# Second layer of a four-layer attention program: its weights split in twelve parts, eight of them during its first round, and two loads issued during the first layer

## The chip, the cores and the metric

The program runs on one core of a Trainium2 chip. The metric is device time in microseconds: the median over repeated executions of the whole program. TensorE is written PE, VectorE DVE, ScalarE ACT, GpSimd POOL and SyncE SP, as the profile does. All loads of this kernel are issued from SP's queue.

## What is computed

Four attention layers follow one another on `x` of shape 16 x 128 x 256, with a context of the same shape. The change is at the start of the second layer (and in what the first layer loads). Cut from the reference, the second layer is:

```python
# z: x after layer one; u: the context; both 16 x 128 x 256, split in two column halves s:e of 128
h = einsum('od,bdl->bol', Wqkv_i, z[:, :, s:e]) + einsum('od,bdl->bol', Winj_i, u[:, :, s:e])
q, k, v = split(concatenate(chunks, axis=2), 3, axis=1)      # 16 heads of 64
score = einsum('bndi,bndj->bnij', q + r_w_bias, k) * SCALE
prob = softmax(score)
attn_vec = einsum('bnij,bndj->bndi', prob, v)
x = einsum('od,bdl->bol', Wo, attn_vec) + bo + z
x = (x - mean(x)) * rsqrt(var(x) + eps)                      # over the 128 channels
```

`Wqkv_i` and `Winj_i` (i = 0, 1) are four matrices of 3072 x 128, 1.5 MB each.

## The kernel before, in words

`program` runs three blocks one after the other, with a barrier between them: `layer0` (layer one), `layer1` (layer two) and `layers23`.

**Layer one** (`layer0`) is a software pipeline over eight pairs of batches. At its start SP issues, in this order (L379 to L390): the first pair's `x_in`, `cols`, `wqkv`, `rows` (broadcast to 128 partitions), `self_mul`, `cT`, `cross_mul`, the other weights, and then three of the four big matrices of layer two: `wz0_raw`, `wz1_raw`, `wi0_raw`. After these it issues `x_in` of pair 1 (`next_x`, L365 to L368), as soon as POOL has made `x_ao` of pair 0 (L436). On DVE the statistics of `x_in` (L824) stand in a fixed order among the score operations (L901, L906); the normalisation `ln` (L837), the copies `vm` (L852) and the transposes of `ln` on PE (L509) come after them.

**Layer two** (`layer1`) works in rounds of two batches, eight rounds, each with sixteen steps (eight pairs of heads times two batches). PE multiplies in a two-term form: every operand of a projection is a rounded high part (suffix `h`, type fp32r, made by ACT) and the remainder (suffix `l`, input minus high part, made by DVE). So before the first projection the weights have to be split: `parts` (L1102) lists eight pieces, the first halves (1536 columns) of the four matrices and then their second halves. ACT rounds them in that order (L1414), DVE subtracts in the same order (L1550), and after the fourth piece both do the same for the context tile `ub` (L1384, L1467). The remainder is written over the raw weight's place (`wz0_raw` and `wzl0` are the same memory).

The fourth matrix, `wi1_raw`, and the first `ub` are loaded by SP at the start of the second layer (L1177 to L1180). Of PE:

```python
for name in AHEAD:          # "q0", "k0", "v0b0"
    pe.wait_ge(lo_made, len(parts) // 2 if name in ("q0", "k0") else len(parts))
    project(0, name)
rounds(pe, body, tail)
```

`project` (L1217) is 12 matmuls for each name: two column halves, times `z` and `u`, times three products of high and remainder parts. The results go to two PSUM banks in turn (`work`, class `Banks`), so `v0b0` waits until DVE has read `q0` out of its bank (`rest_work`, L1454), and the first `scores` (L1235) wait for `k0` (L1458).

A step `t` of a round, in each engine's own order, is written out in the four `body` functions:

- PE (L1309): `scores(t)`, `times_v(t-2)`, `turn(t-1)`, every other step `times_wo`, then the projections listed in `FILLS[t]` (L1112) for later heads.
- ACT (L1389): two exponentials of step t (L1352), `copy_turned(t-1)` (L1361), `round_heads(t-2)` (L1367), the high parts of the projections (L1372, L1375).
- DVE (L1506): `maxima` of both heads (L1427), `copy_turned(t-1)` (L1438), `inverse_sums` (L1433), `rest_heads(t-2)` (L1443), the remainders of the projections (L1454, L1458) or the copy of `v` (L1449).
- POOL (L1199): `norm(t, 0)` and `norm(t, 1)`, which multiply the probabilities by the inverse sums (L1192). PE's `turn(t)` in step t+1 (L1258) waits for them.

The first round has its own unrolled code (`body(0, first=True, ...)`). Before it POOL makes the remainder of `wo` (L1210).

## Time and profile before

| | us |
|---|---|
| median of 3 runs | 1376.34 (1374.86 to 1376.57) |
| the profiled execution's own time | 1375.4 |
| its span, first to last instruction | 1373.7 |
| PE busy | 1246.0 (91%) |
| DVE / ACT / POOL busy | 942.0 / 837.2 / 497.7 |
| last PE instruction of layer one ends | 495.5 |
| first PE instruction of layer two | 506.77 |
| first scores of layer two | 516.42 |

Times inside the trace are microseconds from the start of the span. A row of the timeline has the start, the duration, the engine, the line of the kernel, the operation, what it writes and reads, how many instructions are merged in it, and in brackets how long the engine had been idle and who ended the wait. Back-to-back instructions of one engine overlap a little, so n of them take less than n times the duration of one.

### The profile page before, as it was taken

What the parts mean: (1) busy time and instruction counts of PE and PEld (TensorE: products, weight loads), DVE (VectorE), ACT (ScalarE), POOL (GpSimd) and SP (SyncE); (2) the same over time, 40 slices, a digit from 0 to 9 for tenths busy, and PEclk for the clock granted to TensorE, in tenths of its full rate; (3) what the DMA queues carried; (4) which work ended last, traced back from release to release, by engine and by line L of the source; (5) the groups of instructions that cost most, each with busy time, mean ns of one, the idle gap of its engine ahead of it and who ended that gap; (6) DMA issues with size and microseconds to landing.
All of it is one profiled execution on the core that took longest, in us unless ns stands there. A gap on an engine that the chain in (4) does not pass through costs nothing. (4 is left out here: it accounts for less than half of the span.)

```text
span 1373.7 us, 31155 instructions
## 1 busy us (share of the span) xinstructions
PE 1246.0 (91%) x10866; PEld 1011.5 (74%) x10866; DVE 942.0 (69%) x1843; ACT 837.2 (61%) x2494; POOL 497.7 (36%) x490
## 2 busy tenths in 40 slices
PE   3788999898998749999999999999999999995997
PEld 2667777787787648888888888888888888882554
DVE  2777978879787566666666766666666666662554
ACT  2688877887886545555555555555655556552453
POOL 2455555445544103333333333333333333342000
PEclk9899999999999979999999999999999999997999
DMA  8000000000000020000000000000000000000100
GB/s 312 9 14 20 10 21 8 11 11 16 5 13 1 1 77 1 2 9 1 2 9 0 8 0 0 9 0 0 8 0 9 0 0 1 1 1 26 46 31 31
DMA packets 18547, 24.96 MB, mean 18 GB/s; under 512 B 1360, under 2 KB 16912, under 8 KB 18064
## 3 DMA queue, kind: packets, MB, share of 16 engines
q1 hardware_dynamic: 18448, 23.77, 5.1%
q8 instruction: 46, 0.75, 0.2%
q14 instruction: 53, 0.43, 0.1%
HBM read 21.67 MB, written 2.10 MB: 17 GB/s over the span
## 5 line engine op out<-in xcount | busy, mean ns | idle before, releaser
L1192 POOL TENSOR_TENSOR prob<-prob,l_z_inv 128x512 f32<-128x512 f32 x256 | 261.0, 1040 | 457.1 <-DVE l_z_inv L1433 457.1
L1352 ACT ACTIVATE prob<-psum,l_neg_max 128x256 f32<-128x256 f32 x512 | 235.6, 473 | 245.9 <-DVE l_neg_max L1427 231.9
L741 ACT ACTIVATE ring_e<-ring_e,neg_max 128x128 f32<-128x128 f32 x512 | 164.7, 410 | 15.1 <-DVE neg_max L906 15.0
L1427 DVE TENSOR_REDUCE l_neg_max<-psum 128x2 f32<-128x512 f32 x256 | 164.0, 682 | 10.6 <-PE psum L1246 10.6
L1258 PEld LDWEIGHTS psum<-ident,prob 128*128 128x128 f32 x1024 | 109.8, 141 | 49.0 <-issue 45.4
L1274 PE MATMUL psum<-pT,vs 128*64 128x256 f32 x1024 | 138.8, 391 | 6.7 <-DVE aTl L1443 6.5
L1258 PE MATMUL psum<-ident,prob 128*128 128x128 f32 x1024 | 140.0, 280 | 0.0
L1438 DVE COPY pT<-psum 128x512 f32<-128x512 f32 x128 | 88.2, 689 | 51.1 <-PE psum L1258 51.0
L448 POOL TENSOR_TENSOR ring_e<-ring_e,cross_add 128x512 f32<-128x512 f32 x64 | 83.2, 1308 | 95.2 <-DVE ring_e L901 95.2
L448 POOL TENSOR_TENSOR ring_e<-ring_e,self_add 128x512 f32<-128x512 f32 x64 | 85.4, 1348 | 81.5 <-DVE ring_e L901 80.8
L1443 DVE TENSOR_TENSOR aTl<-psum,aTh 128x256 fp32r<-128x256 f32 x128 | 54.4, 425 | 73.9 <-ACT aTh L1367 73.9
L749 ACT COPY ring_t<-psum 128x512 f32<-128x512 f32 x128 | 75.1, 587 | 48.0 <-PE psum L592 47.3
L1352 ACT ACTIVATION_READ_ACCUMULATOR prob<-psum,l_neg_max 128x1 f32 x512 | 104.0, 203 | 0.0
L1274 PEld LDWEIGHTS psum<-pT,vs 128*64 128x64 f32 x1024 | 63.2, 136 | 42.9 <-issue 5.9
L592 PE MATMUL psum<-ident,ring_e 128*128 128x128 f32 x512 | 83.8, 289 | 8.8 <-ACT ring_t L749 8.8
L1246 PE MATMUL psum<-kh,qh 64*128 64x256 f32 x512 | 85.8, 332 | 4.1 <-ACT prob L1352 4.1
L906 DVE TENSOR_REDUCE neg_max<-ring_e 128x4 f32<-128x512 f32 x128 | 84.7, 666 | 2.0 <-POOL ring_e L448 2.0
L1228 PE MATMUL psum<-zuh,wzh 128*128 128x256 f32 x256 | 74.4, 291 | 11.3 <-DVE zul L1469 11.3
L592 PEld LDWEIGHTS psum<-ident,ring_e 128*128 128x128 f32 x512 | 63.6, 148 | 24.8 <-issue 10.3
L912 DVE RECIPROCAL z_inv<-psum 128x256 f32<-128x256 f32 x32 | 56.1, 1753 | 33.7 <-PE psum L619 33.5
L1361 ACT COPY pT<-psum 128x512 f32<-128x512 f32 x128 | 76.4, 597 | 2.3 <-PE psum L1258 2.3
L1228 PE MATMUL psum<-zuh,wih 128*128 128x256 f32 x256 | 72.8, 284 | 0.0
(197 smaller groups left out, 3226.9 us busy)
## 6 DMA issues: line engine op xcount, KB each, us to landing
wz_raw<-wz_in SPq DMA_DIRECT2D x2, 1536.0 KB, 14.4
x_in<-x SPq DMA_DIRECT2D x8, 256.0 KB, 2.8
cT<-ctxT SPq DMA_DIRECT2D x8, 256.0 KB, 2.9
w<-w_in SPq DMA_DIRECT2D x2, 1024.0 KB, 11.6
l_ub<-ctx_in SPq DMA_DIRECT2D x8, 256.0 KB, 2.7
cg<-ctx_in SPq DMA_DIRECT2D x4, 512.0 KB, 3.7
out<-fin SPq DMA_DIRECT2D x4, 512.0 KB, 2.8
wi_raw<-wi_in SPq DMA_DIRECT2D x1, 1536.0 KB, 17.2
```

The costliest lines, as they stand in the source:

```text
L448: pool.tensor_tensor(e, e, add, ALU.add).then_inc(scores_add.sem, 1)
L592: last = nc.tensor.transpose(turn_bank[:, h * P:(h + 1) * P], ring_e[:, n % RE, h * P:(h + 1) * P], ident[:, :])
L741: last = nc.scalar.activation(e, e, ACT.Exp, bias=neg_max[:, n % RE, h:h + 1])
L906: nc.vector.tensor_reduce(neg_max[:, n % RE, :], ring_e[:, n % RE, :].rearrange("p (h k) -> p h k", h=QUAD), AX.X, ALU.max, negate=True).t ...
L1192: pool.tensor_tensor(e, e, z_inv[:, t % RE, h, :].unsqueeze(2).broadcast_to([P, 2, D]), ALU.mult)\
L1228: last = mm(o, w[wp][c][:, at:at + P], zu[xp][:, s, c, :, :].rearrange("p b l -> p (b l)"), **flags)
L1246: last = mm(score_bank[h][:, qt * D:(qt + 1) * D], q[qp][rows, pair % 2, qt, b, :], k[kp][rows, pair % 2, :, b, :], start=(qp, kp) == (0, ...
L1258: last = nc.tensor.transpose(turn_bank[h][:, kt * D + qt * P:kt * D + (qt + 1) * P], prob[:, t % RE, h, qt * D + kt * P:qt * D + (kt + 1) ...
L1274: last = mm(pv_bank[h * HD1:(h + 1) * HD1, :], vs[:, pair // 2 % 2, b, kt, at:at + HD1], pT[:, h, kt * D:(kt + 1) * D], start=kt == 0, sto ...
L1352: last = nc.scalar.activation(prob[:, t % RE, h, qt * D:(qt + 1) * D], score_bank[h][:, qt * D:(qt + 1) * D], ACT.Exp, bias=neg_max[:, t % ...
L1427: nc.vector.tensor_reduce(neg_max[:, t % RE, h, :], score_bank[h].rearrange("p (t c) -> p t c", t=2), AX.X, ALU.max, negate=True).then_inc ...
L1438: nc.vector.tensor_copy(pT[:, 1, :], turn_bank[1]).then_inc(copied[1].sem, 1)
```

## The change

1. **Loads.** The fourth big matrix (`wi1_raw`, 1.5 MB) joins the other three at the start of layer one, ahead of `x_in` of pair 1. The first `ub` is loaded at the end of SP's list in layer one. To make room, `rows` loses its last 256 columns (its load goes from 1536 to 1280 columns in each of 128 partitions). SP issues neither in layer two any more.
2. **Splitting by parts.** The weights are split in 12 parts of 256 columns of each of the four matrices (`PARTS`): `qk` parts hold the `q` and `k` columns of one pair of heads, `v` parts the columns of four heads. Four parts (`AT_ONCE`) are made before the first round, the other eight in its steps: ACT rounds part t+4 at the end of step t (t = 0 to 7), POOL subtracts its two `wi` pieces after the norms of step t, DVE subtracts its two `wz` pieces in step t+1, between the maxima and `copy_turned`.
3. **Who subtracts.** The remainders of the two `wi` matrices move from DVE to POOL. The two counters are `z_lo_made` and `i_lo_made`.
4. **Who waits.** In the first round every `project` waits for both counters to reach its own part (`rounded`).

```diff
-            for w, src, c in ((wz0_raw, "wz_in", 0), (wz1_raw, "wz_in", 1), (wi0_raw, "wi_in", 0)):
+            for w, src, c in ((wz0_raw, "wz_in", 0), (wz1_raw, "wz_in", 1), (wi0_raw, "wi_in", 0),
+                              (wi1_raw, "wi_in", 1)):
                 sp.dma_start(w[:, :], v[src][c * P:(c + 1) * P, :]).then_inc(l1_weights_in, 16)
...
-            sp.dma_start(rows[:, :], v["rows_in"].partition_broadcast(P)).then_inc(w_rows, 16)
+            sp.dma_start(rows[:, :], v["rows_in"][0:ROWS["bvpg"]].partition_broadcast(P)).then_inc(w_rows, 16)
...
             sp.wait_ge(w_mask, 16)
-            sp.wait_ge(l1_weights_in, 48)
+            sp.dma_start(v["ub"][:, :, :], v["ctx_in"].rearrange("b p d -> p b d")[:, 0:2, :])\
+                .then_inc(v["first_u_in"], 16)
+            sp.wait_ge(l1_weights_in, 64)
+            sp.wait_ge(v["first_u_in"], 16)
...
+        PARTS = ["qk0", "v0", "qk1", "qk2", "v1", "qk3", "qk4", "v2", "qk5", "qk6", "v3", "qk7"]
+        AT_ONCE = 4
+        tensors = ((wz[0][0], wz[1][0], wz0_raw), (wz[0][1], wz[1][1], wz1_raw),
+                   (wi[0][0], wi[1][0], wi0_raw), (wi[0][1], wi[1][1], wi1_raw))
...
-            load_u(0)
-            for h in range(2):
-                sp.dma_start(wi1_raw[:, h * HALF:(h + 1) * HALF],
-                             v["wi_in"][P:2 * P, h * HALF:(h + 1) * HALF]).then_inc(wi_in, 16)
-                sp.wait_ge(wi_in, 16 * (h + 1))
...
+            def rest_part(n):
+                for m, (hi, lo, raw) in enumerate(tensors[2:4]):
+                    pool.wait_ge(hi_made, len(tensors) * n + m + 3)
+                    pool.tensor_tensor(part(lo, n), part(raw, n), part(hi, n).bitcast(F32), ALU.subtract)\
+                        .then_inc(i_lo_made, 1)
...
                     for h in range(2):
                         norm(i, t, h)
+                    if first and t < len(PARTS) - AT_ONCE:
+                        rest_part(t + AT_ONCE)
...
+                if isinstance(i, int) and i == 0:
+                    pe.wait_ge(z_lo_made, rounded(name))
+                    pe.wait_ge(i_lo_made, rounded(name))
...
+            def round_part(n):
+                for hi, lo, raw in tensors:
+                    nc.scalar.copy(part(hi, n), part(raw, n)).then_inc(hi_made, 1)
...
+                    if first and t + AT_ONCE < len(PARTS):
+                        round_part(t + AT_ONCE)
...
                     maxima(i, t, 1)
+                    if first and 0 < t <= len(PARTS) - AT_ONCE:
+                        rest_part(t - 1 + AT_ONCE)
                     if t >= L_T or not first:
                         copy_turned(i, t - L_T)
...
             rest_z(0)
-            for n, (hi, lo, raw) in enumerate(parts):
-                dve.wait_ge(hi_made, n + 1)
-                nc.vector.tensor_tensor(lo, raw, hi.bitcast(F32), ALU.subtract).then_inc(lo_made, 1)
-                if n == 3:
-                    rest_u(0)
+            rest_part(0)
+            rest_u(0)
+            for n in range(1, AT_ONCE):
+                rest_part(n)
```

**How the instructions move on ACT.** The start of layer two, from the rounding of `z` to the first projection read out (`qh`); `wzh`, `wih` are the high parts, `wz_raw`, `wi_raw`, `wil_raw` the weights as loaded. Before:

```order
L1381 CAST zuh<-xs 128x512
L1414 CAST wzh<-wz_raw 128x1536 [waits l1_weights_in]
L1414 CAST wzh<-wz_raw 128x1536
L1414 CAST wih<-wi_raw 128x1536
L1414 CAST wih<-wil_raw 128x1536 [waits l1_wi_in]
L1386 CAST zuh<-l_ub 128x512 [waits l1_u_in]
L1414 CAST wzh<-wz_raw 128x1536 x2
L1372 ACTIVATE qh<-psum,cols 128x512 [waits l1_work_bank0_full]
```

Now:

```order
L1410 CAST zuh<-xs 128x512
L1423 CAST wzh<-wz_raw 128x2x128 x2
L1423 CAST wih<-wi_raw 128x2x128 x2
L1418 CAST zuh<-l_ub 128x512 [waits first_u_in]
L1423 CAST wzh<-wz_raw 128x256 x2
L1423 CAST wih<-wi_raw 128x256 x2
L1401 ACTIVATE qh<-psum,cols 128x512 [waits l1_work_bank0_full]
```

Four casts of 256 columns stand ahead of the rounding of `ub` where four of 1536 did, the wait for `l1_wi_in` is gone, and 16 casts of 256 columns stand ahead of `qh` in all.

**On POOL**, from the barrier into layer two to the norms of the first steps. Before:

```order
L1210 TENSOR_TENSOR wol<-wol_raw,woh 128x1024 [waits wo_hi_made]
L1192 TENSOR_TENSOR prob<-prob,l_z_inv 128x512 [waits l1_z_inv_done] x18
L1197 TENSOR_TENSOR l_rstd<-l_var_eps,half_neg 128x4 [waits l1_work_bank1_read_out]
```

Now:

```order
L1219 TENSOR_TENSOR wil<-wi_raw,wih 128x2x128 [waits weights_hi_made] x2
L1219 TENSOR_TENSOR wil<-wi_raw,wih 128x256 [waits weights_hi_made] x2
L1219 TENSOR_TENSOR wil<-wi_raw,wih 128x2x128 [waits weights_hi_made] x4
L1237 TENSOR_TENSOR wol<-wol_raw,woh 128x1024 [waits wo_hi_made]
L1209 TENSOR_TENSOR prob<-prob,l_z_inv 128x512 [waits l1_z_inv_done] x2
L1219 TENSOR_TENSOR wil<-wi_raw,wih 128x256 [waits weights_hi_made] x2
L1209 TENSOR_TENSOR prob<-prob,l_z_inv 128x512 [waits l1_z_inv_done] x2
L1219 TENSOR_TENSOR wil<-wi_raw,wih 128x2x128 [waits weights_hi_made] x2
```

Eight subtractions stand ahead of the remainder of `wo`, and two after each pair of norms in steps 0 to 7.

**On DVE**, steps 1 and 2 of the first round (`l_neg_max` are the maxima, `pT` is `copy_turned`, `l_z_inv` the inverse sums). Before:

```order
L1427 TENSOR_REDUCE l_neg_max<-psum 128x2 [waits l1_scores_done] x2
L1438 COPY pT<-psum 128x512 [waits l1_pv_done,l1_turned]
L1433 RECIPROCAL l_z_inv<-l_z_sum 128x2 [waits l1_probs_done,l1_exp_done] x2
L1449 COPY vs<-psum 128x512 [waits l1_work_bank1_full]
L1454 SCALAR_TENSOR_TENSOR ql<-psum,cols,qh 128x512 [waits l1_work_hi]
```

Now:

```order
L1462 TENSOR_REDUCE l_neg_max<-psum 128x2 [waits l1_scores_done] x2
L1544 TENSOR_TENSOR wzl<-wz_raw,wzh 128x256 [waits weights_hi_made] x2
L1473 COPY pT<-psum 128x512 [waits l1_pv_done,l1_turned]
L1468 RECIPROCAL l_z_inv<-l_z_sum 128x2 [waits l1_probs_done,l1_exp_done] x2
L1484 COPY vs<-psum 128x512 [waits l1_work_bank1_full]
L1489 SCALAR_TENSOR_TENSOR ql<-psum,cols,qh 128x512 [waits l1_work_hi]
```

Two subtractions stand between the maxima and the inverse sums, in each of steps 1 to 8.

## Rows read from the trace of the kernel before

**Rows 1.** Stretches: length, PE PEld DVE ACT POOL busy, granted clock, DMA share, GB/s.

```profile
496.00:507.00 11.00, 0.23 (x1) 0.26 (x2) 8.55 (x8) 8.98 (x8) 0.00 (x0) 0.57 0.50 167
516.40:606.00 89.60, 88.34 (x769) 74.50 (x768) 62.01 (x131) 52.45 (x175) 33.60 (x33) 0.99 0.01 4
```

**Rows 2.** Timeline of layer two's start, up to its second projection read out.

```profile
496.33 0.62 ACT L1381 CAST zuh<-xs 128x512 fp32r<-128x512 f32 x1 [10.48 <-PEq L150]
496.86 2.84 ACT L1414 CAST wzh<-wz_raw 128x1536 fp32r<-128x1536 f32 x2
496.98 0.69 DVE L1464 TENSOR_TENSOR zul<-xs,zuh 128x512 fp32r<-128x512 f32 x1 [0.96 <-ACT zuh L1381]
...
506.77 0.55 PE L1228 MATMUL psum<-zuh,wzh 128*128 128x256 f32 x1 [11.28 <-DVE zul L1469]
...
511.88 0.60 ACT L1375 ACTIVATE kh<-psum 128x512 fp32r<-128x512 f32 x1 [1.05 <-PE psum L1228]
```

**Rows 3.** The same timeline, the second wait and the first steps.

```profile
513.49 2.38 POOL L1210 TENSOR_TENSOR wol<-wol_raw,woh 128x1024 fp32r<-128x1024 f32 x1 [35.93 <-ACT woh L1420]
513.88 0.68 DVE L1458 SCALAR_TENSOR_TENSOR kl<-psum,kh 128x512 fp32r<-128x512 f32 x1
514.07 0.36 PE L1232 MATMUL psum<-wzh,zuh 128*128 128x256 f32 x1 [2.22 <-DVE wil L1550]
...
518.00 0.41 PE L1228 MATMUL psum<-zuh,wzh 128*128 128x256 f32 x1
```

**Rows 4.** Stretches as in rows 1, around the second wait.

```profile
511.00:512.00 1.00, 0.85 (x6) 0.64 (x5) 1.00 (x2) 0.12 (x1) 0.00 (x0) 0.88 0.10 33
515.00:516.00 1.00, 1.00 (x6) 1.00 (x6) 0.00 (x0) 0.00 (x0) 0.87 (x1) 0.50 0.00 0
```

**Rows 5.** Single casts and subtractions: duration min/median/max in ns.

```profile
L1550 DVE TENSOR_TENSOR wzl<-wz_raw,wzh x4: 1750/1751/1759, 498.4 to 508.2; 128x1536 fp32r<-128x1536 f32 x4
L436 POOL TENSOR_TENSOR x_ao<-x_in,rows x8: 1265/1273/1275, 30.2 to 364.6; 128x512 f32<-128x512 f32 x8
```

**Rows 6.** DVE beside POOL: durations of one line, and the timeline of round seven.

```profile
L1464 DVE TENSOR_TENSOR zul<-xs,zuh x8: 693/1392/1512, 497.0 to 1141.3; 128x512 fp32r<-128x512 f32 x8
...
1140.12 2.04 POOL L1192 TENSOR_TENSOR prob<-prob,l_z_inv 128x512 f32<-128x512 f32 x2 [3.47 <-DVE l_z_inv L1433]
1141.32 1.39 DVE L1464 TENSOR_TENSOR zul<-xs,zuh 128x512 fp32r<-128x512 f32 x1 [0.22 <-ACT zuh L1381]
```

**Rows 7.** Step 2 of the first round: ACT, POOL and PE's turn after it.

```profile
528.09 0.47 ACT L1352 ACTIVATE prob<-psum,l_neg_max 128x256 f32<-128x256 f32 x1 [1.42 <-DVE l_neg_max L1427]
529.77 2.04 POOL L1192 TENSOR_TENSOR prob<-prob,l_z_inv 128x512 f32<-128x512 f32 x2 [3.07 <-DVE l_z_inv L1433]
532.39 1.09 PE L1258 MATMUL psum<-ident,prob 128*128 128x128 f32 x8
```

**Rows 8.** Loads of the first 34 us: KB each, us from issue to landing.

```profile
wi_raw<-wi_in SPq DMA_DIRECT2D x1, 1536.0 KB, 17.2
self_mul<-smask SPq DMA_DIRECT2D x1, 64.0 KB, 7.2
...
x_in<-x SPq DMA_DIRECT2D x1, 256.0 KB, 3.1
```

**Rows 9.** The start of layer one: timeline, and the DMA rate of one stretch.

```profile
16.71 0.43 SPq L390 DMA_DIRECT2D wi_raw<-wi_in  x1
28.00:30.00 2.00, 0.00 (x0) 0.00 (x0) 1.75 (x4) 0.26 (x1) 2.00 (x2) 0.99 1.03 436
31.53 28.78 SPq L354 DMA_DIRECT2D x_in<-x  x2
35.13 0.74 DVE L824 BATCH_NORM_STATS2 stats<-x_in 128x6 f32<-128x256 f32 x2
40.58 0.76 DVE L852 TENSOR_TENSOR vm<-psum,rows 128x256 f32<-128x256 f32 x2 [0.41 <-PE psum L527]
41.49 0.63 PE L509 MATMUL psum<-ident,ln 128*128 128x128 f32 x4 [0.57 <-DVE vm L852]
```

More of the change, by code:

```diff
@@ L101, in program @@
         half_neg = sb("half_neg", [P, 4])
+        ub = sb("l1_ub", [P, 2, D])
+        first_u_in = ctx.enter_context(nc.semaphore("first_u_in"))
         raw_place = ExitStack()
-        wz0_raw, wz1_raw, wi0_raw = (raw_place.enter_context(nc.sbuf_tensor(n, [P, 3 * NQ], F32)) for n in (
-            "wz0_raw", "wz1_raw", "wi0_raw"))
+        wz0_raw, wz1_raw, wi0_raw, wi1_raw = (raw_place.enter_context(nc.sbuf_tensor(n, [P, 3 * NQ], F32)) for n in (
+            "wz0_raw", "wz1_raw", "wi0_raw", "wi1_raw"))
         l1_weights_in = ctx.enter_context(nc.semaphore("l1_weights_in"))
@@ L134, in layer0 @@
         "psum", "xs", "ident", "mean_w", "cols", "half_neg", "col"))
-    (l1_weights_in, wz0_raw, wz1_raw, wi0_raw) = (v[n] for n in ("l1_weights_in", "wz0_raw", "wz1_raw", "wi0_raw"))
+    (l1_weights_in, wz0_raw, wz1_raw, wi0_raw, wi1_raw) = (v[n] for n in (
+        "l1_weights_in", "wz0_raw", "wz1_raw", "wi0_raw", "wi1_raw"))
     NB = 2
@@ L162, in event @@
             return e
-        rows = sb("rows", [P, len(ROWS) * D])
+        rows = sb("rows", [P, ROWS["bvpg"]])
         wqkv = sb("wqkv", [P, 2, 3 * D])
@@ L1044, in layer1 @@
         "sb", "psum", "xs", "ident", "mean_w", "half_neg", "col"))
-    (l1_weights_in, wz0_raw, wz1_raw, wi0_raw, wzl0, wzl1, wil0) = (v[n] for n in (
-        "l1_weights_in", "wz0_raw", "wz1_raw", "wi0_raw", "wzl0", "wzl1", "wil0"))
+    (wz0_raw, wz1_raw, wi0_raw, wi1_raw, wzl0, wzl1, wil0, wil1) = (v[n] for n in (
+        "wz0_raw", "wz1_raw", "wi0_raw", "wi1_raw", "wzl0", "wzl1", "wil0", "wil1"))
     NB = 2
@@ L1073, in place @@
             return raw, sb(name, shape, F32R)
-        wi1_raw, wil1 = place("wil1", [P, 3 * NQ])
         wo_raw, wol = place("wol", [P, PAIRS, P])
@@ L1099, in layer1, with part, rounded @@
         wo_bank = psum[:, 7, :]
[L1101 to L1104 removed]
+        PARTS = ["qk0", "v0", "qk1", "qk2", "v1", "qk3", "qk4", "v2", "qk5", "qk6", "v3", "qk7"]
+        AT_ONCE = 4
+        tensors = ((wz[0][0], wz[1][0], wz0_raw), (wz[0][1], wz[1][1], wz1_raw),
+                   (wi[0][0], wi[1][0], wi0_raw), (wi[0][1], wi[1][1], wi1_raw))
+        def part(w, n):
+            if PARTS[n][0] == "v":
+                return w[:, 2 * NQ + int(PARTS[n][1]) * D:2 * NQ + (int(PARTS[n][1]) + 1) * D]
+            at = int(PARTS[n][2]) * P
+            return w[:, 0:2 * NQ].rearrange("p (t c) -> p t c", t=2)[:, :, at:at + P]
+        def rounded(name):
+            n = "v" + name[1] if name[0] == "v" else "qk" + name[1]
+            return 2 * (PARTS.index(n) + 1)
         wo_hi, wo_lo, wo_in_place = (w[:, :, :].rearrange("p h o -> p (h o)") for w in (*wo, wo_raw))
[L1106 to L1108 removed]
+        wo_in = sem("l1_wo_in")
+        hi_made, z_lo_made, i_lo_made, wo_hi_made, wo_lo_made = (sem(n) for n in (
+            "weights_hi_made", "z_weights_lo_made", "i_weights_lo_made", "wo_hi_made", "wo_lo_made"))
         FILLS = [("q1", "k1"), ("v0b1", "q2"), ("k2",), ("v1b0", "q3"), ("k3", "v1b1"), ("q4", "mean"), ("k4",),
@@ L1207, in tail @@
                 inverse_std(i, "k0")
+            for n in range(AT_ONCE):
+                rest_part(n)
             pool.wait_ge(wo_hi_made, 1)
@@ L1341, in _ @@
             for name in AHEAD:
-                pe.wait_ge(lo_made, len(parts) // 2 if name in ("q0", "k0") else len(parts))
                 project(0, name)
@@ L1384, in round_u @@
             def round_u(i):
-                act.wait_ge(*u_in.at(i))
+                if isinstance(i, int) and i == 0:
+                    act.wait_ge(first_u_in, 16)
+                else:
+                    act.wait_ge(*u_in.at(i - 1))
                 nc.scalar.copy(zu[0][:, 1, :, :, :], ub[:, :, :].rearrange("p b (c l) -> p c b l", c=2))\
                     .then_inc(zu_hi.sem, 1)
+            def round_part(n):
+                for hi, lo, raw in tensors:
+                    nc.scalar.copy(part(hi, n), part(raw, n)).then_inc(hi_made, 1)
             def body(i, first, last):
@@ L1504, in output, with rest_part @@
                 nc.vector.tensor_tensor(to, y[:, b, :], ps, ALU.mult).then_inc(work.reads(name), 1)
+            def rest_part(n):
+                for m, (hi, lo, raw) in enumerate(tensors[0:2]):
+                    dve.wait_ge(hi_made, len(tensors) * n + m + 1)
+                    nc.vector.tensor_tensor(part(lo, n), part(raw, n), part(hi, n).bitcast(F32), ALU.subtract)\
+                        .then_inc(z_lo_made, 1)
             def body(i, first, last):
@@ L1547, in _ @@
             rest_z(0)
-            for n, (hi, lo, raw) in enumerate(parts):
-                dve.wait_ge(hi_made, n + 1)
-                nc.vector.tensor_tensor(lo, raw, hi.bitcast(F32), ALU.subtract).then_inc(lo_made, 1)
-                if n == 3:
-                    rest_u(0)
+            rest_part(0)
+            rest_u(0)
+            for n in range(1, AT_ONCE):
+                rest_part(n)
             for name in AHEAD:
```

22 lines of the change are left out of this document (7 added, 15 removed).

## Prediction

> **What bounds the kernel now.** I read first the stretches, then the timeline of the hand-over from layer one to layer two, then the first round step by step, and last the start of layer one, because a load was moved there. In the stretch of the first round PE is busy 88.3 of 89.6 us, with DVE at 62.0, ACT at 52.5 and POOL at 33.6 [rows 1]. So layer two is bound by PE once it runs, and a round has spare time on the other three. Before it, from 496 to 507, PE is busy 0.23 of 11 us [rows 1]. The reader is to see two waits there: 11.28 us until 506.77, behind the first four pieces of weights, the wait for `wi1_raw` and the context's remainder, and 2.22 us until 514.07, behind the last four pieces on DVE [rows 2, 3]. Both waits are on the path, since PE has nothing else. The second has an after-effect: the granted clock is 0.88 in 511 to 512 and 0.50 again in 515 to 516 [rows 4], 1.2 instead of 2.4 GHz, after the idle stretch from 511.88.
>
> **Prices of the small pieces.** A cast takes 0.62 us for 512 columns (L1381) and two of 1536 take 2.84 [rows 2], so one is 1.47 and the next starts after 1.37. The straight line through both gives 0.41 us for 256 columns, one every 0.31. On DVE 512 columns take 0.69 [rows 2] and 1536 take 1.75 [rows 5], so 256 take 0.42, one every 0.35. On POOL 512 columns with two full inputs take 1.27 [rows 5] and 1024 take 2.38 [rows 3], so 256 take 0.71.
>
> **Term 1: when PE starts.** ACT ends the first cast at 496.95 as now, and its next four are done at 497.27, 497.58, 497.89 and 498.20, the context's at 498.7; no load is waited for. Without any hindrance DVE would end the context's remainder at 499.4 and POOL its second piece at 499.3, and PE would start at 499.5 instead of 506.77. But DVE and POOL now subtract side by side, both with two SBUF inputs. The trace shows what that does: L1464 takes 693 ns at the least and 1392 in the median; at 1141.32 it starts under POOL's pair of norms (1140.12 to 1142.16) and ends 0.55 after the pair does [rows 6]. DVE stood still meanwhile. I therefore put these instructions one behind the other: from 497.6, two pieces on DVE (0.8), the context (0.69), two on POOL (1.42), 2.9 us in all, so PE starts at 500.5, 6.3 us earlier.
>
> The Trainium skill states this as a rule ("SBUF — State Buffer", section "SBUF: two separate sides"): a DVE instruction with two SBUF inputs and a GpSimd instruction take the shared port pair as an exclusive lock, and the later one blocks until the other has ended. The trace agrees (1392 ns beside 693 ns). By it term 1 is 6.3; an even sharing of time would leave up to 7.3.
>
> **Term 2: when the rounds start.** The second half of the wait falls away altogether or nearly. `q0` and `k0` take 5.1 us on PE as now (506.77 to 511.88) [rows 2], so they end at 505.6. `v0b0` waits until DVE has read `q0`, and DVE has six more pieces to do first, which alternate with six of POOL's: 6 x (0.38 + 0.71) = 6.5 us, to 507.0, DVE's last at 506.3. `ql` (0.75) then frees the bank at 507.1, `kl` (0.68) [rows 3] ends at 507.7, `v0b0` runs from 507.1 to 508.6 (24 matmuls in 5.1 us, mostly at half clock, are 0.21 each; my estimate at full clock is 0.12, so 12 take 1.5), the scores take 0.9 to 1.0, and `q1` starts at 509.6, where it starts at 518.00 now [rows 3]: **8.4 us earlier**. The lower bound is half clock through `v0b0` and the scores, as now: the 3.9 us from 514.07 to 518.00 [rows 3] in place of 2.5 gives 7.0. The upper bound is no lock at all: start at 499.5, `k0` at 504.6, `v0b0` at once to 506.1, scores, `q1` at 507.1, 10.9 earlier. I take 8.4, which goes by the row nearest to the case (rows 6). POOL then has the remainder of `wo` (2.38) from 507.0 to 509.4 and its first norm at about 511.6, so that is hidden.
>
> **Term 3: the eight parts inside the first round.** ACT gets four casts (1.3 us) at the end of steps 0 to 7. Before the exponentials of step 2 it idles 1.42 us [rows 7], and in the same view the other seven steps have about as much or more: it fits, by about 0.1. DVE gets 0.8 us between maxima and inverse sums in steps 1 to 8, plus the wait for POOL's two pieces, which become ready only just before: about 0.5. So the norms of a step come some 1.1 us later. Those of step 2 end at 531.81, and `turn` begins at 532.39 and needs the second head half of its 1.09 later, at 532.9 [rows 7]: 1.1 us late against 1.1 us of slack. In the same view this is the tightest of the eight steps. POOL idles 3.07 before these norms [rows 7] and its two pieces need 1.4. Nothing else of PE hangs on it: the parts are made at least one step before their projection. I take +0.3 us, with 0 and 3 as bounds (0.3 to 0.4 lost in each of eight steps, if the slack is used up). The work is the same number of columns; only its cover, PE's 99% busy round, is new. If that cover went, it would cost 8 x 1.3 us on ACT.
>
> **Term 4: the moved loads.** Layer two's own issues go (what ACT waited for them lies inside term 1), and the first `ub` is loaded while SP has nothing to do: 0. But `wi1_raw` is now queued ahead of `x_in` of pair 1. The rows show that what is queued is served behind what was issued before: `self_mul`, 64 KB, lands 7.2 us after its issue behind `rows`, and `wi_raw`, issued at 16.71, after 17.2 us, at 33.9 [rows 8, 9]. `x_in` is issued at 31.53 and lands 3.1 later, at 34.6; DVE takes it at 35.13 with no wait [rows 8, 9]. Now 1.57 MB more and 0.13 MB less (`rows`) stand before it, 1.44 MB at 436 GB/s [rows 9]: 3.3 us. It lands at about 38.0 and DVE's statistics are 2.9 late. Behind them on DVE stand the scores' masks and maxima, `ln` and `vm`, all in order. `vm` has 0.41 us of slack (it waited for PE), and PE waits 0.57 for it before the transposes at 41.49 [rows 9]. So PE is 2.5 late from there, and this pipeline only starts up: I find nothing later that it could catch up on. **+2.5 us.** Bounds: 0, if PE's work in hand covers it, and 4, if PE's longer idleness costs clock as well. That `self_mul` comes 0.4 us earlier behind the shorter `rows` does not help, since the wait for `x_in` follows.
>
> **Sum.** -8.4 + 0.3 + 2.5 = -5.6 us, from the profiled execution's 1375.4 to 1369.8. The median of the runs is 0.9 above that execution, so the median to come is 1376.3 - 5.6 = 1370.7. About 0.2% (2.75 us) is what a measurement tells from no change.
>
> **Rivals.**
> - *DVE and POOL do not hinder each other.* Then term 2 is 10.9 and the sum -8.1: 1368.2. For it: in the first pieces DVE is done before POOL starts, and pieces of 256 columns are short. Against it: rows 6. Chance 0.13.
> - *The late `x_in` costs nothing* (served earlier than I think, or caught up). Then the sum is -8.1 as well, 1368.2, or 1366 with the rival above. For it: `x_in` landed after 3.1 us although `wi_raw` was still under way. Against it: every load of this queue lands in its turn. Chance 0.15.
> - *Half clock at both places*: term 2 is 7.0, term 4 is 4, sum -2.7: 1373.6. For it: rows 4 show it once after a gap of 2.2 us; mine are 1.5 and some 2. Chance 0.15.
> - *Slower: POOL is the new bound.* Mechanism: a POOL piece of 256 columns (half of them as 2 x 128) costs as much as one of 512, 1.27. Then four parts at the start take 8 x 0.56 = 4.5 us longer, and in each of eight steps the norms come 2.2 us late; against 1.1 us of slack in the tightest and more in the others I count 0.6 us of PE each, 5 in all. Sum: -8.4 + 4.5 + 5 + 2.5 = +3.6, 1379.9. It decides from about 0.4 us of additional cost in each piece on. Against it: POOL's 1.27 and 2.38 lie on a line that leaves 0.16 for zero columns. Chance 0.05.
> - *The change does not do what it says*, because the second wait merely moves to DVE's backlog; that is inside term 2 and has been priced there.
>
> **Chances and range.** My forecast has 0.52, the rivals 0.13, 0.15, 0.15 and 0.05. Faster by over 0.2% are the forecast, the first two rivals and nearly half of the third: 0.86. Within 0.2%: 0.10; slower: 0.04. The range is 1366.3 to 1374.0: down to both fast rivals together, up to the half clock at both places.
>
> **What would show it.** In the changed profile: PE's first projection at about 500.5 + 2.5 = 503 (if it is 502, the lock is not there); POOL's pieces near 0.7 us or stretched by DVE's; `q1` about 6 us before 518.00; DVE idle before the statistics near 35 until `x_in` lands near 38, and layer one's last matmul at 498 instead of 495.5; the first round still 99% PE busy and no new wait of PE on POOL's norms. I am wrong if layer one ends where it did (term 4), if the time from layer one's end to `q1` shrinks by other than 8.4 (term 2), or if the first round takes over 1 us longer (term 3).

## The result, and the profile after

The changed kernel takes 1384.45 us in the median (1382.86 to 1385.85, 6 runs), the kernel before 1375.9 in the same comparison: ratio 1.0063, 95% interval [1.005, 1.0076]. It is **slower by 0.6%**, some 8.5 us, where 5.6 us less was forecast, and the range ended at 1374.0. The profiled execution took 1385.29, its span is 1383.6.

| From the two traces (us) | before | after | difference |
|---|---|---|---|
| `xs`, last of layer one on DVE, starts | 495.60 | 501.32 | +5.7 |
| from there to the first `q1` matmul | 22.40 | 12.53 | -9.9 |
| from `q1` to the end of the span | 855.7 | 869.75 | +14.05 |
| span | 1373.7 | 1383.6 | +9.9 |

**The entry of layer two** did what was forecast, and more. Timeline of the changed kernel:

```profile
501.32 0.42 DVE L898 SCALAR_TENSOR_TENSOR xs<-psum,x_mlp 128x256 f32<-128x256 f32 x1 [3.04 <-PE psum L535]
502.04 0.62 ACT L1410 CAST zuh<-xs 128x512 fp32r<-128x512 f32 x1 [10.47 <-PEq L154]
503.66 7.37 POOL L1219 TENSOR_TENSOR wil<-wi_raw,wih 128x256 fp32r<-128x256 f32 x8 [20.39 <-ACT wih L1423]
505.12 5.32 DVE L1544 TENSOR_TENSOR wzl<-wz_raw,wzh 128x256 fp32r<-128x256 f32 x6
505.88 0.55 PE L1258 MATMUL psum<-zuh,wzh 128*128 128x256 f32 x1 [4.67 <-POOL wil L1219]
511.35 0.36 PE L1262 MATMUL psum<-wzh,zuh 128*128 128x256 f32 x1 [0.40 <-DVE ql L1489]
513.85 0.39 PE L1258 MATMUL psum<-zuh,wzh 128*128 128x256 f32 x1
```

The trace shows every wait in brackets at the end of its row. Against [rows 2, 3], PE's first wait is 4.67 us instead of 11.28 and its second 0.40 instead of 2.22, and both have other releasers. DVE's six subtractions take 5.32, POOL's eight 7.37: about 0.9 us each, in step with each other.

**The start of layer one**, changed kernel:

```profile
38.16 0.75 DVE L832 BATCH_NORM_STATS2 stats<-x_in 128x6 f32<-128x256 f32 x2 [3.38 <-DMA x_in<-x]
41.54 1.71 DVE L845 TENSOR_SCALAR ln<-x_in,mean_var,rstd 128x256 f32<-128x256 f32 x2
43.17 0.74 DVE L860 TENSOR_TENSOR vm<-psum,rows 128x256 f32<-128x256 f32 x2
44.06 1.09 PE L517 MATMUL psum<-ident,ln 128*128 128x128 f32 x4 [3.80 <-DVE vm L860]
49.71 1.76 DVE L920 RECIPROCAL z_inv<-psum 128x256 f32<-128x256 f32 x1 [4.61 <-PE psum L627]
```

`x_in` lands at 38.1 and PE's transposes start at 44.06 instead of 41.49 [rows 9], 2.6 late. Then the clock doubles the damage. Stretches of the changed kernel, then of the one before (length, PE PEld DVE ACT POOL busy, granted clock, DMA share, GB/s):

```profile
44.00:46.00 2.00, 1.94 (x12) 1.64 (x16) 1.10 (x2) 0.00 (x0) 0.00 (x0) 0.50 0.00 0
46.00:48.00 2.00, 2.00 (x24) 1.06 (x28) 0.00 (x0) 1.96 (x5) 0.00 (x0) 0.50 0.00 0
48.00:50.00 2.00, 2.00 (x36) 1.46 (x28) 0.29 (x1) 0.70 (x3) 0.00 (x0) 0.61 0.00 0
```

```profile
44.00:46.00 2.00, 1.13 (x21) 0.73 (x14) 1.44 (x1) 2.00 (x8) 0.00 (x0) 1.00 0.00 0
46.00:48.00 2.00, 2.00 (x12) 1.82 (x12) 0.74 (x2) 1.38 (x5) 0.00 (x0) 1.00 0.00 0
```

Behind the stop of 3.80 us PE runs at 1.2 GHz for over 4 us where it ran at 2.4. The `RECIPROCAL` behind it starts at 49.71 instead of 44.56: 5.15 late, about what layer one's end shows.

**The loop of rounds 1 to 6** is where the time went, and nothing in my text had looked there. The six rounds are six passes through one loop in PE's code, with five taken branches between them. One stretch of it, changed kernel and then kernel before:

```profile
700.00:800.00 100.00, 96.56 (x838) 81.16 (x837) 66.66 (x141) 57.87 (x190) 35.59 (x36) 1.00 0.02 4
```

```profile
700.00:800.00 100.00, 98.89 (x861) 83.22 (x859) 68.15 (x146) 59.80 (x197) 37.66 (x37) 1.00 0.01 3
```

PE's waits from 603 to 1240 (line waited for, us in total, times, longest), changed kernel and kernel before:

```profile
PE psum L1276 <- DVE vs L1484: 12.4, 5, 2.8
PE psum L1304 <- DVE aTl L1478: 2.2, 7, 0.3
PE psum L1276 <- ACT prob L1381: 1.9, 7, 0.4
```

```profile
PE psum L1274 <- DVE aTl L1443: 4.1, 15, 0.3
PE psum L1246 <- ACT prob L1352: 3.7, 14, 0.3
```

Five waits of 2.5 us, one for each time that the loop's branch is taken, at the first scores behind it. The timeline around the first of them, changed kernel:

```profile
690.88 0.28 PE L1262 MATMUL psum<-wil,zuh 128*128 128x256 f32 x1
693.42 0.38 PE L1276 MATMUL psum<-kh,qh 64*128 64x256 f32 x2 [2.25 <-DVE vs L1484]
...
694.32 1.66 PE L1304 MATMUL psum<-pT,vs 128*64 128x256 f32 x8
695.91 1.97 PE L1288 MATMUL psum<-ident,prob 128*128 128x128 f32 x8
```

The scores do not read `vs`: the named releaser is only the last event before. After the stop eight matmuls of L1304 take 1.66 us and eight of L1288 1.97, where the latter took 1.09 [rows 7]; the granted clock is 0.50 from 695 to 697. The view of the DMA queues had one more difference. The queues that carry instructions, 700 to 800, changed kernel and kernel before (packets, MB, share of 16 engines):

```profile
q8 instruction: 10, 0.16, 0.8%
```

```profile
q14 instruction: 5, 0.04, 0.1%
```

In this stretch the changed kernel has no packet of q14 and the kernel before none of q8. Queue q8 brings 16 KB a packet. In the kernel before it brings seven packets in the loop's first pass (595 to 685) and none from 686 to 1150. In the changed kernel it goes on with about nine in every further pass; over the whole program it has 91 packets against 46. Around each of the five stops the packets lie alike: two start 0.8 to 2.2 us before PE stands still (689.03 and 690.06, the stop from 691.16), and a third just after it goes on (693.79).

The count of instructions comes from the built programs, not from a trace: PE's loop has 1,708. A pass of the kernel before takes 91.25 us, and q8's packets in its first pass come 13.8 us apart, so a packet holds about 258 instructions, 64 bytes each by this estimate, and the loop is some 109 KB, 6.7 packets. **Theory F**: PE's loop is fetched anew in every pass, because its place in the code moved. The loop itself is as long as before; the first round's extra waits, two counters in each of 24 projections, put 24 instructions ahead of it (two waits share an instruction in the built program). **Theory M**, the rival: the split parts, the new places of the weights, or contention slow the rounds.

Queue q14, with 8 KB a packet, behaves the other way round: 34 packets from 603 to 1230 in the kernel before, five in each pass, and 7 in the changed kernel. It is not PE's, since experiment 1, where only PE's code moves, leaves it at 33. So an engine other than PE fetched code in every pass of the kernel before, and PE waited at most 0.35 us at a time there (603 to 1235).

### The profile page after: what moved, and what is told of

Read it like the earlier page. It is cut to its first block and busy times, and to the rows that moved or that the text cites. A ratio compares the mean times of both kernels' runs of the same rounds, so it can differ in the third digit from the quotient of the medians.

```text
span 1383.6 us, 31258 instructions
## 1 busy us (share of the span) xinstructions
PE 1250.9 (90%) x10866; PEld 1014.4 (73%) x10866; DVE 938.9 (68%) x1859; ACT 843.0 (61%) x2534; POOL 518.0 (37%) x514
## 5 line engine op out<-in xcount | busy, mean ns | idle before, releaser
L1381 ACT ACTIVATE prob<-psum,l_neg_max 128x256 f32<-128x256 f32 x512 | 236.0, 473 | 235.5 <-DVE l_neg_max L1462 235.4
L1288 PEld LDWEIGHTS psum<-ident,prob 128*128 128x128 f32 x1024 | 111.8, 142 | 49.9 <-issue 45.6
L1304 PE MATMUL psum<-pT,vs 128*64 128x256 f32 x1024 | 140.4, 395 | 5.6 <-DVE aTl L1478 5.4
L1288 PE MATMUL psum<-ident,prob 128*128 128x128 f32 x1024 | 142.2, 283 | 0.0
L1381 ACT ACTIVATION_READ_ACCUMULATOR prob<-psum,l_neg_max 128x1 f32 x512 | 103.7, 203 | 0.0
L1276 PE MATMUL psum<-kh,qh 64*128 64x256 f32 x512 | 85.6, 330 | 15.3 <-DVE vs L1484 12.4
L1304 PEld LDWEIGHTS psum<-pT,vs 128*64 128x64 f32 x1024 | 63.7, 137 | 41.9 <-issue 7.0
L1276 PEld LDWEIGHTS psum<-kh,qh 64*128 64x128 f32 x512 | 48.1, 184 | 37.4 <-issue 21.0
```

The costliest lines, as they stand in the source:

```text
L1276: last = mm(score_bank[h][:, qt * D:(qt + 1) * D], q[qp][rows, pair % 2, qt, b, :], k[kp][rows, pair % 2, :, b, :], start=(qp, kp) == (0, ...
L1288: last = nc.tensor.transpose(turn_bank[h][:, kt * D + qt * P:kt * D + (qt + 1) * P], prob[:, t % RE, h, qt * D + kt * P:qt * D + (kt + 1) ...
L1304: last = mm(pv_bank[h * HD1:(h + 1) * HD1, :], vs[:, pair // 2 % 2, b, kt, at:at + HD1], pT[:, h, kt * D:(kt + 1) * D], start=kt == 0, sto ...
L1381: last = nc.scalar.activation(prob[:, t % RE, h, qt * D:(qt + 1) * D], score_bank[h][:, qt * D:(qt + 1) * D], ACT.Exp, bias=neg_max[:, t % ...
```

## The experiments

A pair (a, b) says by how many instructions PE's loop starts and ends later than in the kernel before; the changed kernel is (24, 24). These counts come from the built programs, not from the traces. A satisfied wait is a wait for a count that the semaphore has long reached: it holds nothing up and only takes its place in the code.

**1. The kernel before with 24 instructions more: (24, 24).**

```diff
+            for _ in range(48):
+                pe.wait_ge(l1_weights_in, 48)
             for name in AHEAD:
                 pe.wait_ge(lo_made, ...)
```

> The kernel before, with 48 waits that are long satisfied put on PE ahead of layer two's first projections (two share one instruction: 24 instructions more, as many as the changed kernel has). Nothing else differs. Theory F (instruction fetch: PE's loop of rounds 1 to 6 is as long as before, 1,708 instructions of 64 bytes, but lies 24 instructions further on, and so touches one 16 KB block of code more and is fetched anew in each round): some 14 us slower than the kernel before (1387 to 1392), 9 or 10 packets of the instruction queue q8 in each 100 us of the loop where the kernel before has none, and PE standing still 2.3 to 2.8 us once per round at the first L1268 matmuls behind the loop's branch. Theory M (the rounds got slower by the change's own work: the split parts, the places of the weights in SBUF, or contention): the time of the kernel before (1375 to 1377), no packets in the loop. Both: the 24 instructions themselves lie in PE's wait of 11 us and cost under 1 us.

Measured: 1390.03 us, ratio 1.0096 [1.0081, 1.0111]. Its waits from 603 to 1240:

```profile
PE psum L1246 <- DVE vs L1451: 12.5, 5, 2.7
```

and its instruction queue over the program:

```profile
q8 instruction: 91, 1.49, 0.5%
```

With none of the change's work in it, it has the changed kernel's picture: five stops, 12.5 us against 12.4, and 91 packets. The median is 14.0 us above that of the kernel before (1376.06 in this comparison); in the trace, from `q1` to the end it takes 871.9 us instead of 855.7. Theory M falls for this cost.

**2. The changed kernel moved further: (244, 244).**

```diff
+            for _ in range(440):
+                pe.wait_ge(l1_weights_in, 48)
             for name in AHEAD:
                 project(0, name)
```

> The changed kernel with 440 waits that are satisfied (220 instructions) on PE ahead of layer two's first projections, where PE waits 4.67 us. They move PE's loop past the next 16 KB boundary, to where it starts 8 to 32 instructions into a block and fits seven blocks again. Theory F: rounds 1 to 6 lose the stop of 2.3 to 2.8 us and the lower clock behind it: 1384.5 - 14 = 1370.5, up to 6 us more if the pads are executed slower than PE waits there (1369 to 1377); q8 packets in the loop 0. Theory M: 1384 to 1390, the rounds as slow as in the changed kernel.

Measured: 1390.22, ratio 1.0096 [1.0082, 1.0111]. The time is outside what I gave for F, but the loop does what F says. PE's start in the timeline, and a stretch of the loop:

```profile
526.99 0.55 PE L1258 MATMUL psum<-zuh,wzh 128*128 128x256 f32 x1 [25.06 <-issue]
```

```profile
1000.00:1100.00 100.00, 98.85 (x855) 82.85 (x852) 69.14 (x149) 59.86 (x199) 36.78 (x37) 1.00 0.01 3
```

The rounds are whole again: there is no stop behind a branch, q8 is back to 47 packets, and from `q1` to the end it takes 855.6 us, where the changed kernel took 869.7 and the kernel before 855.7. All of the loop's 14 us come back with more code ahead of it, not less. The added waits cost what hides this in the time: PE starts at 526.99 instead of 505.88, 0.7 of which came earlier. I had allowed 6 us. The 20.4 us that are left make 46 ns for each of 440 waits, and that is the least, because part of them ran while PE would have waited for POOL anyway. Counted from the start of layer two (`zuh` at 502.76) they took at most 24.2 us, 55 ns each.

**3. Half the extra waits: (12, 12).** Only the first user of a part waits.

```diff
-                if isinstance(i, int) and i == 0:
+                if isinstance(i, int) and i == 0 and (name[0] == "q" or name[2:] == "b0"):
                     pe.wait_ge(z_lo_made, rounded(name))
                     pe.wait_ge(i_lo_made, rounded(name))
```

> The changed kernel in which only the first projection that uses a part of the weights waits for it (q names, and the first half of each v): 12 of the 24 extra instructions go, and PE's loop lies 12 further on than in the kernel before. Theory F: either the boundary lies in the last 12 of the 24, then all 14 us come back (1369 to 1372, no q8 packets in the loop), or in the first 12, then nothing (1384 to 1385, 9 to 10 packets per 100 us as now). Nothing between the two. Theory M: 1384 +- 1, with or without packets. A theory that the waits themselves cost time in the first round: at most 12 x 0.06 = 0.7 us back.

Measured: 1372.52 in the median, but 12 runs from 1370.7 to 1383.59; ratio 0.9987 [0.997, 1.0004]. "Nothing between the two" was wrong: in the profiled run two of the five branches are followed by a stop (2.5 and 3.3 us) and three are not, with 64 packets of q8 in all. At this place the same code stops behind some branches and not behind others.

**4. The input of pair 1 first.**

```diff
-            for ... in (..., (wi0_raw, "wi_in", 0), (wi1_raw, "wi_in", 1)):
+            for ... in (..., (wi0_raw, "wi_in", 0)):
...
                 if g < R0:
                     next_x(g)
+                if g == 1:
+                    sp.dma_start(wi1_raw[:, :], v["wi_in"][P:2 * P, :]).then_inc(l1_weights_in, 16)
```

> The changed kernel with the load of the fourth weight tensor issued behind the input of pair 1 instead of ahead of it. The late input is the whole cause of layer one's later end (501.3 against 495.6): 5.7 us back, 1384.5 - 5.7 = 1378.8 (1378 to 1380), x_in landed by 35.2, DVE's last L890 near 495.6. If the later end has another cause (the larger tensors, the load of the next layer's input): under 1 us back. The loop's stops (2.3 to 2.8 us in each of the rounds 1 to 6) stay as in the changed kernel.

Measured: 1379.39, ratio 1.0025 [1.0014, 1.0037]; 5.1 us better than the changed kernel. PE's wait before the transposes is 0.6 us again, not 3.8, the clock is 1.00 from 44 to 50, and layer one ends where it did or earlier (the other traces with this repair, experiments 6, 7 and 15, have `xs` at 494.87 to 496.61, the kernel before 495.60):

```profile
494.65 0.42 DVE L899 SCALAR_TENSOR_TENSOR xs<-psum,x_mlp 128x256 f32<-128x256 f32 x1 [3.04 <-PE psum L536]
```

Its loop lies at (24, 24) and has the five stops (12.4 us) still. So the two costs are separate.

**5. The first round's code made no longer than before: (-11, -11).** As in 3, and the wait for the turned inputs, satisfied from `q0` on, is left out at the first round's other projections.

```diff
-                pe.wait_ge(*zu_lo.at(i, 1))
+                if not (isinstance(i, int) and i == 0) or name == "q0":
+                    pe.wait_ge(*zu_lo.at(i, 1))
```

> The changed kernel with PE's code of the first round made as short as before: only the first user of a part waits for it, and the wait for the turned inputs stands once, ahead of q0, instead of at each of the first round's projections (it is satisfied from then on). PE's loop lies 11 instructions nearer to the start than in the kernel before; the work is that of the changed kernel. Theory F: no q8 packets in the loop, no stop behind its branch, 1384.5 - 14 = 1370.5 (1369 to 1372), and without the scatter of the run with half the waits (1370.7 to 1383.6). Theory M: 1384.

Measured: 1370.79 (1369.91 to 1372.28), ratio 0.9969 [0.9958, 0.9979]. A stretch of its loop:

```profile
700.00:800.00 100.00, 98.85 (x856) 83.12 (x856) 68.35 (x146) 59.75 (x198) 37.28 (x37) 1.00 0.01 3
```

q8 has 46 packets in the whole program, as in the kernel before. The removal of satisfied waits brings 13.7 us back by the medians, 12.9 by the ratios to the kernel before in each comparison. From `q1` to the end it takes 856.3 us, 0.6 more than before the change.

**6. Both repairs.** The edits of 4 and 5 together.

> The run before with the fourth weight tensor loaded behind the input of pair 1 as well. The two costs are in different places and add: 1384.5 - 14 - 5.1 (the measured gain of x_in first) = 1365.4 (1364 to 1367), faster than the kernel before by 10 to 11, which is what layer two's earlier entry measures in the trace (21.67 us from its start to the first q1 projection before, 11.81 now). If the entry's gain is given back later: 1370 to 1375.

Measured: 1366.51 (1364.68 to 1367.48), ratio 0.9934 [0.992, 0.9948]. The time is the one expected, but the gain on the kernel before is 8.6 us, not 10 to 11. The trace shows where the rest of the entry's 10.0 us (12.41 from `xs` to `q1`, instead of 22.40) is: `xs` comes 1.0 later and the stretch from `q1` to the end is 0.7 longer, both small beside what separates single traces (`xs` of experiments 5 and 2 lies 0.8 before and 0.7 after that of the changed kernel, whose first layer they share). This version beats both kernels.

**7. Who hinders whom.** On 6, DVE makes all sixteen remainders ahead of the first projections.

```diff
-            for n in range(AT_ONCE):
-                rest_part(n)
             pool.wait_ge(wo_hi_made, 1)
...
             def rest_part(n):
-                for m, (hi, lo, raw) in enumerate(tensors[0:2]):
+                for m, (hi, lo, raw) in enumerate(tensors if n < AT_ONCE else tensors[0:2]):
...
-                        .then_inc(z_lo_made, 1)
+                        .then_inc(z_lo_made if m < 2 else i_lo_made, 1)
```

> The run before, with all 16 subtractions ahead of layer two's first projections on DVE and none on POOL. Theory L (DVE and POOL hinder each other: 0.89 and 0.92 us each while both work, 0.35 to 0.42 for DVE alone): DVE's subtractions take 0.35 to 0.42 again, part 0 is whole 1.3 us earlier, PE starts 1.3 us earlier after the layer's start (2.5 instead of 3.8), and ql no longer stands behind them: 1.3 to 2.5 us faster than the run before. If 0.89 us is what these operands cost DVE (halves of strided rows): 16 x 0.89 = 14.2 us of subtractions, ql 4 us later, 3 to 5 us slower.

Measured: 1365.14 (1364.0 to 1366.35), ratio 0.9926 [0.9912, 0.9939]; the intervals of 6 and 7 overlap. The subtractions ahead of the first round, experiment 7 and then the changed kernel (busy us, mean ns):

```profile
L1544 DVE TENSOR_TENSOR wzl<-wz_raw,wzh 128x256 fp32r<-128x256 f32 x8 | 3.0, 414 | 0.0
L1544 DVE TENSOR_TENSOR wil<-wi_raw,wih 128x256 fp32r<-128x256 f32 x8 | 3.0, 413 | 0.0
```

```profile
L1544 DVE TENSOR_TENSOR wzl<-wz_raw,wzh 128x256 fp32r<-128x256 f32 x8 | 6.1, 817 | 0.0
L1219 POOL TENSOR_TENSOR wil<-wi_raw,wih 128x256 fp32r<-128x256 f32 x8 | 7.4, 954 | 20.4 <-ACT wih L1423 20.4
```

The same instruction takes 414 ns alone and 817 beside POOL; DVE does all sixteen in 6.0 us, less than the 6.1 in which it did eight. POOL's help was worth nothing here. PE starts 0.4 us sooner after `xs` than in 6, not 1.3, because the context's remainder stands behind part 0 on DVE (it ends at 500.25, PE starts at 500.40); `q1` comes 0.75 sooner. Theory L holds. The medians give 1.4 us, the lower end of the 1.3 to 2.5 that I expected, but with overlapping intervals; the entry itself gives 0.75, about half.

**8 to 14. Where must the loop lie?** First the kernel before with the edit of experiment 1, but 24 waits (12 instructions), the place of experiment 3:

> The kernel before with 24 satisfied waits (12 instructions) on PE ahead of layer two's first projections: its loop lies where that of the changed kernel with half the waits did. Theory F: the same picture as there, some rounds with the stop and others without, runs that scatter from 1376 to 1389, more than the 1374.8 to 1378.1 of the kernel before. If the scatter there came of the change's work: 1376 +- 1 as before.

Measured: 1382.55 (1380.11 to 1386.78), ratio 1.0048 [1.0033, 1.0063], three stops of 3.4 us, 73 packets. Some branches have the stop and some not, as in 3, without the change's work.

Then start and end were moved apart, on the base of 6, by satisfied waits ahead of the loop (N of them) and in it (M a step), or by leaving out the wait for the turned inputs in the loop too (23 instructions less). N and M were 72 and 0 with the shorter loop, and then 0 and 5, 70 and 5, 0 and 9, 70 and 0, 46 and 5:

```diff
             for t in range(STEPS):
...
+                for _ in range(M if not isinstance(i, int) else 0):
+                    pe.wait_ge(l1_weights_in, 48)
                 for name, r in fills(i, t, last):
...
-                if not (isinstance(i, int) and i == 0) or name == "q0":
+                if name == "q0":
                     pe.wait_ge(*zu_lo.at(i, 1))
...
+            for _ in range(N):
+                pe.wait_ge(l1_weights_in, 48)
             for name in AHEAD:
```

> The kernel with no longer code and x_in first, in which the wait for the turned inputs is left out in the loop too, but at its first user (PE's loop is 23 instructions shorter, 1,685), and 72 satisfied waits stand ahead of layer two's first projections: the loop starts 23 instructions later than in the kernel before (the changed kernel: 24) and ends where it ended before. Theory F1 (what counts is how many 16 KB blocks the loop touches, so where it ends): no q8 packets in the loop, no stop behind the branch; the time is that of the run without the pads (1366.5) plus what the 36 pad instructions cost on PE's queue, up to 3 us: 1365 to 1370. Theory F2 (what counts is where it starts): 9 to 10 packets per 100 us and +14 us, 1380 to 1384.

> The kernel with no longer code and x_in first, with satisfied waits spread over the steps of the loop alone (33 instructions more): the loop starts 11 instructions earlier than in the kernel before and ends 22 later (the changed kernel: 24 later). The packets are the verdict, since 33 instructions per round may themselves cost up to 3 us a round. Theory F1 (the end): 50 or more packets of q8 between 603 and 1240, and a stop of 2.3 to 3.6 us behind the branch in most rounds, time over 1378. Theory F2 (the start): 12 to 16 packets there and no stop, time 1366 to 1385 by what the pads cost.

> The kernel with no longer code and x_in first, 70 satisfied waits ahead of layer two's first projections (35 instructions) and 33 instructions of them in the loop: starts 24 later and ends 57 later than in the kernel before. If a late start is needed and a late end as well (what fits all runs so far): some 56 q8 packets between 603 and 1240 and the stop behind the branch. If the boundary lies just behind an end of 22 and only the end counts: the same. If the waits in the loop are what kept the code in place: no packets.

> The same base, no waits ahead, 65 instructions more in the loop: it starts 11 earlier and ends 54 later than in the kernel before. If the end counts, and its boundary lies behind 22: some 56 packets and the stop. If a late start is needed as well: 11 to 13 packets, no stop.

> The same base with 70 satisfied waits ahead alone: start and end 24 later than in the kernel before, as in the changed kernel. Theory F: some 56 packets, the stop in all rounds, 1366.5 + 14 = 1380 and up to 3 us for the pads. If there are no packets, this base differs in something else, and the position isn't the cause.

> The same base with 46 waits ahead (23 instructions) and 33 instructions in the loop: starts 12 later, ends 45 later. If a late start is needed, from between 0 and 12 on: packets in some of the rounds or in all, 20 to 56. If only a late end beyond 22 is needed: 56.

| (start, end) | on | stops in 5 branches | q8 packets, 603 to 1230 | median us |
|---|---|---|---|---|
| (0, 0) | kernel before | 0 | 12 | 1375.9 |
| (-11, -11) | changed | 0 | 12 | 1370.79 |
| (-11, -11) | 6 | 0 | 13 | 1366.51 |
| (23, 0) | 6, shorter loop | 0 | 11 | 1365.15 |
| (-11, 22) | 6, longer loop | 0 | 13 | 1367.99 |
| (12, 12) | kernel before | 3 | 38 | 1382.55 |
| (12, 12) | changed | 2 | 30 | 1372.52 |
| (12, 45) | 6, longer loop | 3 | 38 | 1373.74 |
| (24, 24) | kernel before | 5 | 56 | 1390.03 |
| (24, 24) | changed | 5 | 56 | 1384.45 |
| (24, 24) | 6 | 5 | 56 | 1379.92 |
| (24, 57) | 6, longer loop | 5 | 57 | 1376.59 |
| (-11, 54) | 6, much longer loop | 5 | 57 | 1383.15 |
| (244, 244) | changed | 0 | 12 | 1390.22, some 20 of it added waits |

Packets and stops go together in every row: in the nine traces with stops, each of the 38 stops has two packets of q8 that start 0.5 to 2.7 us before it and one within 1 us after it, and the branches without a stop have none. The medians are those of each run, on three bases; on one base five stops cost 1379.92 - 1366.51 = 13.4 us, the 70 waits ahead included. With waits added in the loop as well the same count of stops stands beside 10.1 us (24, 57) and 16.6 us (-11, 54), and these runs do not tell why. The rule of the place is not found. "The end alone" (F1) explains (23, 0) but not why (-11, 22) is quiet beside (12, 12); "the start alone" (F2) is contradicted by (23, 0) and by (-11, 54), and "both must be late" by (-11, 54). The three kernels that stop only sometimes all start at 12, and (244, 244) is quiet again. A count of the 16 KB pieces that the loop touches does not fit either: the loop of (-11, 22) covers all the places of (12, 12) and more, and was quiet. This stays open, and so does where in a piece the loop starts, since the trace does not show the address of the code.

The Trainium skill ("Runtime: NRT & Kernel Launch", section "Instruction fetch mechanics") says that a taken branch whose target is outside the current window of two pages forces a DMA fetch of the target before execution goes on. The traces agree in part: the stops and the extra packets lie at the taken branches, though two of these packets start before PE stands still. But by a window of two pages of 16 KB every round of the kernel before would have fetched, and q8 brought nothing from 686 to 1150 in a loop of some 109 KB: there the measurement decides. The same section gives 2,048 instructions for PE's store, and the loop's 1,708 would be inside that.

**15. The shorter loop, on 7.**

> The kernel with DVE alone (1365.1), with the wait for the turned inputs left out at all of the loop's projections but the first: 23 instructions less per round on PE. If PE's matmuls wait for its queue of instructions anywhere in the loop: up to 23 x 0.045 = 1 us a round, 6 us in all, 1359 to 1364. If the queue runs ahead of PE (PE is 98.9% busy in the loop): 1365 +- 1.

Measured: 1364.11 (1363.29 to 1365.37), ratio 0.9918 [0.9904, 0.9931]. It is 1 us from experiment 7, inside both intervals. PE is 98.86 of 100 us busy from 700 to 800, as without it. So 23 instructions a round are worth nothing that these runs can measure, which fits the second expectation. It has the lowest median of all (its interval overlaps those of experiments 6 and 7 and of (23, 0)), **0.8% faster than the kernel before**, and 1.4% faster than the changed kernel (0.9918 / 1.0063 = 0.9856).

## Why the prediction was wrong, point by point

- **Term 1, right.** From `zuh` (L1381, now L1410) PE's first projection came after 10.44 us and now after 3.84: 6.6 earlier, forecast 6.3. The releaser is POOL, as the order one behind the other wants.
- **Term 2, right in mechanism, too small in size.** 9.9 us instead of 8.4. It was mis-sized in `v0b0` and what leads to `q1`: PE's second wait was 0.40 us, and from 511.35 to `q1` it took 2.50 as forecast, but the forecast began `v0b0` 6.6 us after PE's start (500.5 to 507.1) where it measured 5.47. A pair of pieces, one of DVE's and one of POOL's, took 0.92 (7.37 / 8), not 0.38 + 0.71 = 1.09; with DVE's 0.41 alone, that leaves an estimated 0.51 for POOL's piece. The rival without hindrance falls with experiment 7.
- **Term 3, right within its bounds.** +0.3 forecast. From `q1` to the end it is +0.6 and +0.7 in experiments 5 and 6 (856.3 and 1365.4 - 509.02 = 856.4, against 855.7) and -0.1 in experiment 2, so it is not told from nothing. PE's waits in the first round stayed near 1 us (0.6 and 0.5, as before). The rival with POOL as the bound did not come about.
- **Term 4, right in mechanism, half in size.** `x_in` landed at 38.1 (38.0 forecast) and PE was 2.6 late (2.5 forecast). The step that failed is "4, if PE's longer idleness costs clock as well" as the upper bound, and 2.5 as the choice: at `RECIPROCAL` PE's 2.6 had become 5.15, at half clock in between, so the clock cost as much again as the wait. Measured: 5.7 in the trace, 5.1 by the medians of experiment 4. The half clock behind a gap stood in rows 4 for layer two; here I had it only in the bound, and that was too low.
- **The step that decided** is in term 3: "The work is the same number of columns; only its cover ... is new", and in what was left out: the waits that I counted at nothing. The change adds 24 instructions to PE ahead of a loop whose own code it does not touch, and I costed the loop of rounds 1 to 6 at zero without a sentence on it. Experiments 1, 2 and 5 show +14 us by the loop's place alone. No row of the kernel before has this price, since q8 brings nothing in the loop there. But its DMA view shows q14 with five packets in every pass, so that code can be fetched anew in every pass was to be read there, and should have made a rival for the 24 instructions. What decides which place is quiet stays open.
- **The range** went "down to both fast rivals together", which is -10.9 + 0.3 = -10.6 and so 1365.7; it was given as 1366.3. This changes nothing here.
- **The slower rival** ended at 1379.9, by another mechanism, and had 0.05. The sum with the measured terms: -9.9 + 5.7 + 14.05 = +9.9, the difference of the spans; whatever term 3 cost is inside the last.

## What to carry to other kernels

When an engine's loop is large (here 1,708 instructions on PE), instructions added ahead of it, even waits that are always satisfied, can make every pass fetch its code again. When time appears at a loop's start and the named releaser has no data for the waiting instruction, compare the packets of the instruction queues inside the loop between the two traces first. Leave out waits that an earlier wait on the same engine covers; here that alone turned 0.6% slower into 0.3% faster. It is no rule for a quiet place, though: 12 instructions more were worse than none, and 244 more were quiet. Price an idle gap of PE with the clock behind it: here 2.6 us of lateness became more than 5.

## What the runs showed of the hardware

- In the kernel before, PE ran a loop of 1,708 instructions (some 109 KB) with no packet on q8 from its second pass on. With the loop 24 instructions further on, q8 brought about nine packets of 16 KB in each pass, and PE stood still for 2.3 to 2.8 us at each taken branch; 12 further on, this happened at some branches and not at others; 244 further on, at none.
- Code was fetched in every pass without PE standing still: q14 brought five packets of 8 KB a pass in the kernel before, for an engine other than PE. What it cost that engine was not looked at.
- A satisfied wait on PE cost 46 to 55 ns where the engine had nothing in hand (440 of them: 20.4 to 24.2 us), and nothing measurable inside a round that was 98.9% busy (experiment 15).
- DVE took 414 ns for a subtraction of 256 columns alone and 817 while POOL did the same kind; the two engines together finished sixteen later (POOL's last at 511.03, 9.0 us after `zuh` starts) than DVE alone (504.3, 7.3 us after it).
